# A two-layer attention kernel: the mean of the queries comes from ScalarE's copy, GpSimd masks the heads, and every engine gets a new order

## The reference

```python
# layer 0: x is (256, 512); 8 heads of 32; keys, queries and values are the same projection
q = x.T @ Wq.T
logits = (scale * qh @ qh.T * cmask + (1 - cmask) * NEG) * rmask
x = x + ((softmax(logits) @ qh) @ Wo.T).T
# layer 1: 256 rows of width 512; 16 heads of 32
xn = rms_norm(x, g_norm) * (1 + scale_c) + shift_c
q, k, v = split(xn @ W_qkv);  q, k = rms_norm(q, g_q), rms_norm(k, g_k)
o = softmax(q @ k.T * 32 ** -0.5) @ v
x = x + o + o @ W_out
```

## Time and profile before

| | |
|---|---|
| runs | 1326.3 us median of 3 (1326.19 to 1329.03) |
| profiled execution | 1324.62 us, its span 1322.8 us |
| busy in the span | PE 1261.4 us (95%), DVE 1055.8 (80%), ACT 774.6 (59%), POOL 764.4 (58%) |
| granted clock of TensorE | 0.972 of full speed over the span |
| chain that ended last | PE 88%, ACT 4%, DVE 2% |

### The profile page before, as it was taken

The page is one execution under the profiler, slowest core; times in us unless marked ns, Lnnn a source line. Parts: engine busy times, 40 slices in busy tenths (PEclk is TensorE's granted clock), DMA queues, the critical chain, the costliest instruction groups (busy, mean ns, idle before and its releaser), DMA issues.

```text
span 1322.8 us, 20986 instructions
## 1 busy us (share of the span) xinstructions
PE 1261.4 (95%) x6896; PEld 597.6 (45%) x6896; DVE 1055.8 (80%) x934; ACT 774.6 (59%) x1377; POOL 764.4 (58%) x389
## 2 busy tenths in 40 slices
PE   6969899999999999999999999999999999999987
PEld 4424444444444454444445444444444444444433
DVE  6756778888887887888788788878888887888654
ACT  1626565665656566565656666565666656566523
POOL 0337467475746747484674748467474856638452
PEclk8859899999999999999999999999999999999999
DMA  8321534525264452626445252634525263441322
GB/s 288 105 65 47 136 105 96 140 54 151 74 148 109 99 138 56 149 72 150 107 107 131 60 147 70 153 104 112 130 60 145 69 156 100 113 110 44 97 59 70
DMA packets 77962, 143.03 MB, mean 108 GB/s; under 512 B 21536, under 2 KB 23072, under 8 KB 77856
## 3 DMA queue, kind: packets, MB, share of 16 engines
q1 hardware_dynamic: 69136, 126.17, 38.1%
q10 hardware_dynamic: 8720, 15.51, 4.0%
HBM read 32.02 MB, written 8.39 MB: 31 GB/s over the span
## 4 chain that ended last, share of the span: by engine, by line
PE 88%; ACT 4%; DVE 2%; issue 2%; SPq 1%; ACTq 1%; POOL 1%; DMA 0%; DVEq 0%
PE PX L541 25%; PE PS L453 11%; PE PO L480 9%; PE PX L575 8%; PE PO L502 5%; PE PS L467 4%; PE PX L398 4%; PE PM L422 4%; PE PX L519 2%; PE PM L491 2%; PE PM L519 2%; PE PM L559 2%; PE PM L431 2%; PE PO L505 2%; ACT E L1055 2%
## 5 line engine op out<-in xcount | busy, mean ns | idle before, releaser
L1048 ACT ACTIVATE E<-PS,KBIAS 128x512 f32<-128x512 f32 x512 | 345.3, 686 | 236.8 <-PE PS L453 221.9
L541 PE MATMUL PX<-WQKV,XNT 128*128 128x512 f32 x768 | 382.4, 602 | 3.4 <-ACT QK L1026 2.1
L1948 POOL TENSOR_TENSOR E<-E 128x1024 f32<-128x1024 f32 x112 | 263.4, 2359 | 160.8 <-PE PO L480 92.9
L1565 DVE TENSOR_REDUCE NM<-PM 128x4 f32<-128x2048 f32 x128 | 291.3, 2276 | 52.3 <-PE PM L422 52.3
L453 PE MATMUL PS<-B,A 97*128 97x512 f32 x512 | 301.7, 624 | 5.3 <-ACT E L1048 4.9
L1978 POOL TENSOR_TENSOR KQLO<-E 128x1024 f32<-128x1024 f32 x64 | 151.2, 2363 | 211.3 <-ACT E L1055 209.5
L1960 POOL TENSOR_TENSOR RQK<-RQK,HALF 128x16 f32<-128x16 f32 x64 | 201.0, 3148 | 28.3 <-DVE RQK L1653 27.5
L1572 DVE TENSOR_REDUCE NM<-PM 128x8 f32<-128x2048 f32 x64 | 146.6, 2291 | 49.1 <-PE PM L431 49.0
L541 PEld LDWEIGHTS PX<-WQKV,XNT 128*128 128x128 f32 x768 | 137.8, 192 | 91.4 <-issue 75.7
L1055 ACT ACTIVATE E<-PS 128x512 f32<-128x512 f32 x256 | 145.3, 596 | 49.0 <-PE PS L467 48.3
L453 PEld LDWEIGHTS PS<-B,A 97*128 97x128 f32 x512 | 95.6, 192 | 148.1 <-issue 123.6
(11 more groups left out here) (84 smaller groups left out, 1408.2 us busy)
## 6 DMA issues: line engine op xcount, KB each, us to landing
A<-QHI SPq DMA_DIRECT2D x256, 64.0 KB, 2.0
B<-QHI SPq DMA_DIRECT2D x256, 64.0 KB, 2.0
A<-KQHI SPq DMA_DIRECT2D x128, 128.0 KB, 2.3
B<-KQHI SPq DMA_DIRECT2D x128, 128.0 KB, 2.4
XB<-x SPq DMA_DIRECT2D x16, 512.0 KB, 3.9
A<-QLO SPq DMA_DIRECT2D x128, 64.0 KB, 2.0
B<-QLO SPq DMA_DIRECT2D x128, 64.0 KB, 2.0
X<-x ACTq DMA_DIRECT2D x16, 512.0 KB, 5.4
```

Of the source, the lines that this page charges most:

```text
L541: last = mm(PX[:, :], XNT[:, c, t * P:(t + 1) * P], WQKV[:, c, part * DM:(part + 1) * DM], start=(c == 0), stop=(c == 3))
L1048: fn(E[:, probs(seg, i, g), h, :], PS[n % 2][:, :], ACT.Exp, bias=KBIAS[:, g, b:b + 1], scale=SCALE).then_inc(exp_done, 1)
L1565: v.tensor_reduce(NM0[:, q, :].rearrange("p (h k) -> p h k", k=KB0)[:, :, kb], PM[:, :, :], axis=AX.X, op=ALU.max, negate=True).then_inc(m ...
L1948: g_.tensor_tensor(running(seg, i)[:, heads_, :], running(seg, i)[:, heads_, :], E[:, probs(seg, i, g), heads_, :], ALU.add).then_inc(done, 1)
```

## The change

`sums_x`, both `mask_x`, `project_mean` and `mean0` go. `project0` waits only for the load of x. `take_query` sums its row into `QSUM` while it copies (`accum_out`). POOL's new `mask_query` multiplies `QF` by the mask in place, and `round_query` and PE's `values0` wait for it. The factor 1/512 moves into `masked_out`, which now gives (1 - mask)/512, and `take_sums0` multiplies by 512 times as much. All orders are new, in the tables too. The diff, cut to its core:

```diff
             def project0(i, b, mt):
-                pe.wait_ge(xm_done.sem, xm_done.at(b))
+                pe.wait_ge(xin_in.sem, xin_in.at(b))
...
-            def project_mean(i, b):
...
             def values0(i, b, mt):
                 bank = small(("t0", mt), i)
-                pe.wait_ge(big_taken, BIG.upto(("p0", mt), i - 1))
+                pe.wait_ge(masked.sem, masked.at(b, mt + 1))
...
-                copy(QF[:, mt, :], PX[:, :]).then_inc(big_taken, 1)
+                fn(QF[:, mt, :], PX[:, :], ACT.Copy, accum_out=QSUM[:, mt, b:b + 1]).then_inc(big_taken, 1)
...
             def round_query(i, b, mt):
-                act.wait_ge(big_taken, BIG.upto(("p0", mt), i))
+                act.wait_ge(masked.sem, masked.at(b, mt + 1))
...
-            def mask_x(i, b):
+            def mask_query(i, b, mt):
                 pool.wait_ge(cbm_in.sem, cbm_in.at(b))
-                pool.wait_ge(xs_done.sem, xs_done.at(b))
-                for c in range(2):
-                    g_.tensor_tensor(XB[:, c, :], XB[:, c, :], CBM[:, :], ALU.mult).then_inc(xm_done.sem, 1)
+                pool.wait_ge(big_taken, BIG.upto(("p0", mt), i))
+                g_.tensor_tensor(QF[:, mt, :], QF[:, mt, :], CBM[:, :], ALU.mult).then_inc(masked.sem, 1)
```

On the other engines, in the parts that follow `out0` and around the pieces:

```diff
 # ACT
+                if l1:
+                    take_heads(i, i - 1, 3)
                 if l0:
                     rows0(i, i, 1)
                 if l1:
-                    take_heads(i, i - 1, 3)
                     square_heads(i, i - 1, 3)
...
+                if l1:
+                    keep_x1(i, i - 1)
+                if l0:
+                    load_residual(i, i)
+
+                step_c(0, 0)
...
 # DVE
                 if l0:
-                    add_keys0("A", i, 2, False)
                     add_keys0("A", i, 3, False)
+                    add_keys0("A", i, 3, True)
...
                 if p0:
                     maxima0(i, i + 1, 0, 3)
+                if l1:
+                    invert1(i, i - 1, 0)
                 if l0:
                     norm(i, i)
...
 # POOL
                 if l1:
                     add_keys1(i, i - 1, 0)
                     add_keys1(i, i - 1, 1)
+                    add_keys1(i, i - 1, 2)
                 if l0:
                     rstd(i, i)
-                if l1:
-                    add_keys1(i, i - 1, 2)
```

More of the change, by code:

```diff
@@ L662, in iteration @@
                 if l1:
-                    heads_rows(i, i - 1, 0)
                     heads_rows(i, i - 1, 1)
-                if p0:
-                    project0(i, i + 1, 1)
+                if l0:
+                    values_weighted0("A", i, 0, 3)
+                    weights_summed0("A", i, 0)
                 step_b(0, 2)
-                if l0:
-                    weights_summed0("A", i, 0)
-                step_b(0, 3)
-                step_b(1, 0)
                 if l1:
@@ L675, in iteration @@
                     heads_rows(i, i - 1, 3)
[L676 to L679, removed]
+                step_b(0, 3)
+                step_b(1, 0)
                 if p0:
-                    project_mean(i, i + 1)
+                    project0(i, i + 1, 1)
                 if l1:
                     maxima1(i, i - 1, 0)
-                step_b(1, 3)
+                step_b(1, 1)
                 if l0:
                     values_weighted0("B", i, 1, 0)
-                step_b(2, 0)
-                step_b(2, 1)
+                step_b(1, 2)
                 if o1:
@@ L767, in iteration @@
                 step_c(3, 2)
+                if l1:
+                    values_and_sums1(i, i - 1, 2)
                 step_c(3, 3)
@@ L1300, in iteration @@
                 step_c(2, 3)
+                if l1:
+                    take_context1(i, i - 1, 1)
+                step_c(3, 0)
+                if p0:
+                    rows0(i, i + 1, 0)
+                step_c(3, 1)
                 if l0:
                     norm(i, i)
-                step_c(3, 0)
-                step_c(3, 1)
+                step_c(3, 2)
                 if p0:
-                    rows0(i, i + 1, 0)
-                step_c(3, 2)
-                if l1:
-                    take_context1(i, i - 1, 1)
+                    round_query(i, i + 1, 1)
+                step_c(3, 3)
                 if l0:
                     modulate(i, i)
-                step_c(3, 3)
                 if l1:
@@ L1320, in iteration_before @@
                 take_query(i, i + 1, 1)
+                round_query(i, i + 1, 1)
                 rows0(i, i + 1, 0)
-                mean0(i, i + 1)
-                round_query(i, i + 1, 1)
             def iteration_0(i):
@@ L1361, in iteration_0 @@
                 exp0("B", i, i, 2, 3)
+                take_query(i, i + 1, 1)
                 exp0("B", i, i, 3, 0)
-                mean0(i, i + 1)
-                round_query(i, i + 1, 1)
                 exp0("B", i, i, 3, 1)
@@ L1688, in iteration @@
                 l0, l1, p0, o1 = has(i, 0), has(i, -1), has(i, 1), has(i, -2)
-                if p0:
-                    sums_x(i, i + 1)
                 if o1:
                     invert1(i - 1, i - 2, 2)
+                if l0:
+                    maxima0(i, i, 1, 0)
                 if l1:
@@ L1706, in iteration @@
                     maxima0(i, i, 1, 2)
+                    add_keys0("A", i, 1, False)
                 if l1:
@@ L2005, in iteration @@
                 if l0:
+                    masked_out(i, i)
+                if p0:
+                    mask_query(i, i + 1, 0)
+                    mask_query(i, i + 1, 1)
+                if l0:
+                    add_keys0("B", i, 1, True)
                     add_keys0("B", i, 1, False)
-                    add_keys0("B", i, 1, True)
+                    add_keys0("B", i, 2, False)
                     add_keys0("B", i, 2, True)
-                    add_keys0("B", i, 2, False)
                     add_keys0("B", i, 3, True)
```

547 lines of the change are left out of this document (262 added, 285 removed), and 12 rows, old and new, of tables (BIG, special).

## The result

The changed kernel takes 1337.92 us (median of 4 runs, 1335.58 to 1340.87), the kernel before 1326.64 us (4 runs). The ratio is 1.0082 with a 95% interval of 1.0059 to 1.0106: slower by 0.8%, where 1314 was forecast, and outside the range of 1303 to 1332. The profiled execution took 1335.58 us with a span of 1333.8, which is 11.0 more than the span before.

What follows compares the result with a forecast made beforehand. PE's own work was taken as the period: -1.0 us in each of fourteen iterations (-14.0), +2.0 at the start, -0.5 at the end, so -12.5 on 1324.6: 1312.1 profiled, median 1314. Own range 1307 to 1321, full range 1303 to 1332.

Steps and rivals of the forecast that it cites:

- The step that failed: Last qk to heads_rows 2: power 3 starts before DVE's add and takes 2.90 us, so PE has no wait.
- rival A: At piece 3, POOL's power waits for DVE's add; heads_rows 2 0.9 us late each iteration, 1326.6 us; chance 0.17.
- -0.98 per iteration: On PE's path: removing project_mean's eight one-column records saves 0.98 us in each iteration.
- -0.13: heads_rows 2 to out0's end: weights_summed0 and values_weighted0 together in stage A, the second costing 0.86 us instead of 0.99.
- +0.20: heads_rows 2 to out0's end: c8 between maxima0 2 and values_and_sums1 0, first score pair costs 0.43 instead of 0.24 us.
- +0.25: heads_rows 2 to out0's end: PE waits 0.25 us at maxima1 3 for DVE to reduce maxima1 2.
- -0.35: After out0: 7.93 us to the next iteration instead of 8.28, the take_context1 wait going and POOL's add late next.
- The start: Iterations -1 and 0: about +2 us together (between -2 and +5), +1.2 to the first score, second projection +2.3, mean -1.5.
- The end: Iterations 15 to 17: masked_out out of piece 3's chain -0.4, last stack -0.8, values_and_sums1 3 +0.7, together -0.5 us.
- Rival B: Start of C: ACT stands at keep_x1 for a late store; at 1.8 us late +1.4 per iteration, 1333 us; chance 0.19.
- Rival C: The counted waits, 0.25 us at maxima1 3 and 0.38 for POOL's add, do not come: 1305 us; chance 0.10.
- Rival D: The mean was hidden: PE then waits for DVE and loses all of the 1.0 us, about 1327 us; chance 0.04.

Runs made afterwards that it cites:

- e2: The changed kernel with DVE's context1 3 ahead of the two adds of A3 in iterations 1 to 14: 1329.43 us, ratio 1.0020.
- c3: The changed kernel with the moves of e2 and e4, keep_x1 behind the first C exponential, and weights_summed0 of A behind score b2: 1321.57 us, ratio 0.9962.
- m1: The changed kernel with eight one-column matmuls (two records each) put back on PE in iterations 1 to 14: 1371.18 us, ratio 1.0345.
- b1: The kernel before with the new way to form the mean, old orders kept on every engine: 1331.31 us, ratio 1.0040.
- b2: As b1, but in iteration 0 POOL masks half 1 only after the adds of B1 and B2: 1330.69 us, ratio 1.0036.
- c2: The changed kernel with e2, e4, keep_x1 behind C's first exponential; iteration 0's second projection, take_query 1 and half-1 mask near their old places: 1322.64 us, ratio 0.9974.
- e4: The changed kernel with batch 15's mask load issued by SP in iteration 14, ahead of the stacks of half 1: 1336.60 us, ratio 1.0071.
- e3: The changed kernel with ACT's square of piece 3 ahead of rows0 and POOL's power 3 ahead of piece 2's normalising, iterations 1 to 14: 1386.15 us, ratio 1.0445.
- s1: The changed kernel with the orders of the kernel before in iterations -1 and 0 on all engines: 1346.29 us, ratio 1.0153.
- b3: As b2, with POOL also masking half 0 ahead of its first two adds in iteration 0: 1324.69 us, ratio 0.9994.

## Why the prediction was wrong

*The step that failed* is in the stretch from the last `qk` to `heads_rows` 2: "POOL's power starts 3.07 us after the `qk`", and DVE's add "0.15 later than the power starts. So I take 2.90". The power started 3.37 us after it, 0.15 behind the add, and took 3.84. The 0.30 is DVE's `add_eps` beside POOL's normalisings, which I had at 0.17, though the earlier trace rows show the like on DVE's norm. With 0.15 us of margin a term of 0.33 turned the case over. The forecast had PE there at 7.2 us, PE came at 8.39: 1.2 us in each iteration, some 17 of the 23.5 us between the forecast and the profiled execution. The margin was named, and rival A had the right mechanism at 0.17. Of the 1.2 us, 1.03 are PE's wait (0.9 in rival A), and the rest is PE's own work up to there, 7.36 us where I had 7.2. A margin of 0.15 us on a sum of five engine steps deserved an even chance at least, and I had counted the two rows as equals: in the kernel before the power took 3.81 us in 13 of the iterations 1 to 14, and the row at 513.95 is the only one with 2.90. e2 shows the cause: with the order of starts changed the wait goes, and 8.5 us come back. That is 0.7 to 0.8 of the 1.2 us. The rest stays even in c3, where piece 3 is there 7.5 us after the last `qk`: the forecast's 7.1 and 7.2 were too short by themselves.

*The mean.* -0.98 per iteration held in the new order (m1: 1.78 of 1.84 us exposed). It did not hold in the old one, where the same removal gave 0.2 to 0.25 (b1, b2), for the columns lay ahead of a wait for `split1` 3. I had taken it that work on the chain is worth its length. It is worth that only as far as what comes next is ready.

*The other steps of the period* (-0.13, +0.20, +0.25, -0.35) came out within 0.1 us as sums of their stretches. One by one they did not: the wait of 0.25 us at `maxima1` 3, which I had named as a sign, is not there (PE has no idle time above 0.1 us at it in iterations 2 to 13), and the wait for POOL's add is 0.18 us instead of 0.38. What made up for that in the sums no run took apart.

*The start.* +2.0 was forecast. It is +3.1 in the mean of ten profiles against two, 1.2 ahead of iteration 0 (1.2 forecast) and 1.8 in it; the first profile, with +4.2, was one of the long ones. The late second projection, which I had taken as the cause in iteration 0, was not shown to be it: c2 moved it and gained nothing. The low clock has a part in the spread: in six of the ten profiles the granted clock over iteration 0 is 0.71, and it takes 64.2 to 65.4 us; in the other four it is 0.68, and it takes 66.2 to 67.3. The kernel before has 63.7 us at 0.69. Whether the orders set the clock or the clock falls by chance stays open. The price of 3.2 us for a projection was also taken from a place outside iteration 0 (15 us): in iteration 0 of the kernel before the two took 2.65 and 1.88 us, in the changed kernel 3.24 and 3.65.

*The end.* -0.5 was forecast, with `masked_out` out of the chain. I hadn't followed SP's queue: the last split is later, so the stacks, so the mask load behind them, and `masked_out` came back into the chain at 5.66 us of idle time. That is 2.4 us in e4's profile against this one. The rest of the 5.2 us between forecast and profile is one more period's miss of 1.2, and some 1.6 that no run took apart.

*Rival B* had the right place. The store was met late in some iterations, by 0.2 to 0.7 us at PE, never by the 1.4 that it needed. *Rival C* was right about the two waits, in part, and wrong about the time. *Rival D* is half true: the mean was for the most part hidden in the orders of before.

The condition that I took from two rows of the trace stands in the Trainium skill too, on another page than the one that the prediction names (SBUF - State Buffer, Who interferes with whom): a VectorE instruction with two inputs in SBUF contends with a GpSimd instruction that reads SBUF, and it is the order of issue that decides who blocks. (That the first has the shared ports for the whole instruction, the section says of VectorE's 2-port modes.) The runs agree: 3.84 us when the add was first, 2.90 in e3 when it was not, and 3.01 in e2, where only the last 0.25 us of a multiplication were ahead.

## What to carry to other kernels

Work on the critical chain is worth its length only if the next thing that is waited for is ready; look what it hides before you count it. Where a forecast hangs on which of two engines starts first by 0.1 or 0.2 us, put both orders into the sum, and let the order of instructions decide it (a short operation between) instead of the durations. A move on one engine makes an event late, and it is the queues behind that event, DMA issues above all, that have to be followed to their end, also in the iterations that are written out by hand; a new wait in front of a queue (b1, s1, b2) can cost several times what the operation itself does (7.0 us of iteration 0 between b1 and b3, for the places of two masks of 1.3 and 2.2 us).

## What the runs showed of the hardware

POOL's power is held by an add or a multiplication of DVE (two inputs in SBUF) that began before it, and not by one that begins after it. It takes 2.90 us when it is first (e3), 3.84 when DVE's add of 1.2 us began 0.15 before it, and 3.01 behind the last of a multiplication of 0.41. Not every operation of DVE holds it. In seven profiles (before, after, b1, e2, e3, m1, c3) more than a hundred powers of the four pieces began while DVE was reducing maxima out of PSUM, with up to 2.1 us left, and 17 while it took a reciprocal, with up to 1.6 us left, and all of them took 2.9 us. One such pair, iteration 15 of the changed kernel:

```profile
1219.25 1.74 DVE L1637 RECIPROCAL T<-T 128x256 f32<-128x256 f32 x1
1220.27 2.90 POOL L1922 TENSOR_TENSOR RQK<-RQK,HALF 128x16 f32<-128x16 f32 x1
```

The other way round DVE's `add_eps` took 0.50 instead of 0.17, and its multiplication in e3 1.27 instead of 0.41, both beside POOL's normalisings. The numbers fit a late starter that waits for the end of the other's single instruction: 596.50 + 1.22 + 2.90 = 600.62 against 600.49, and in e2 591.20 + 0.41 + 2.90 = 594.51 against 594.37. No run here had one such pair alone.

One-column matmuls cost what the earlier trace rows show, and sixteen of them behind a wait of 1.03 us came with a granted clock of 0.83 over 10 us (of which 3.3 us are at 0.50, that is 1.2 GHz, and the rest at 2.4) where it was 1.00 before and after them. It was so in each of the three iterations of m1 that took 1.7 us more and in iteration 14; in nine others the same work went by without a fall, as at 770 to 780 us, where the clock stayed at 1.00.
